# A fused four-layer kernel: in an attention turn, the second unit's values are weighed ahead of the last block's projection

## The chip, the cores and the metric

The kernel runs on one core of one Trainium2 chip. The metric is the device time in microseconds (us) of one execution, as the median of several runs. Three runs of the kernel before gave 1235.06, 1235.08 and 1236.01 us: a median of 1235.08 us. One further execution was recorded by the profiler; all rows below come from it.

The core has five engines that run their own instruction streams and meet only at semaphores: TensorE (PE in the rows; its weight loads are PEld), VectorE (DVE), ScalarE (ACT), GpSimd (POOL) and the queue of SyncE (SP).

## The reference, cut to what matters

The input x has 16 batches of 256 rows and 256 columns. It goes through four residual layers: a cross-attention to a context of 77 rows, a mixture of experts, a second cross-attention block with its own feed-forward part, and a last feed-forward layer. The change concerns the two attentions, which are computed by the same code. Of the first one:

```python
Q = _split_heads(q @ Wq.T + bq)      # q: layernorm(x), 16 heads of 16 columns
K = _split_heads(k @ Wk.T + bk)      # k, v: the context
V = _split_heads(v @ Wv.T + bv)
scores = jnp.einsum('bhnd,bhmd->bhnm', Q, K) / jnp.sqrt(jnp.float32(D))
scores = jnp.where(mask == 0, -jnp.inf, scores)
attn = jax.nn.softmax(scores, axis=-1)
out = jnp.einsum('bhnm,bhmd->bhnd', attn, V)
out = out.transpose(0, 2, 1, 3).reshape(q.shape[0], q.shape[1], H)
return out @ Wp.T + bp
...
x = x + jnp.tanh(g_xattn[0]) * _L0_xattn_ref(_layernorm(x, axis=-1), ctx_1024, ...)
```

## The kernel before, in words

An attention stage (stage 0 and stage 1) handles its 16 batches as 16 blocks of 256 rows, one after the other. The work of a block is cut into four units j = 0 to 3: one half of the heads (8 heads) by one half of the rows (128 rows). For each unit, TensorE multiplies queries with keys (`score`, L866), VectorE takes the maximum of each row and head (`score_max`, L471) and subtracts it (`less_max`, L476), ScalarE takes the exponential, TensorE transposes the probabilities (`transpose_prob`, L882), ScalarE copies the transposed ones out of PSUM (`transposed`, L724, the instruction of L728), TensorE weighs the values with them (`weigh_values`, L890), and VectorE divides by the sums (`normalise`, L485). When the four units of a block are done, TensorE transposes the result (`transpose_o`), ScalarE and VectorE split it in a high and a low part, TensorE multiplies it with the output weights (`project`, L912, twelve matmuls on L798 to L800), and VectorE adds the product to the residual stream (`residual`, L501: the instruction of L506 in stage 0, of L511 in stage 1).

The order of the work is written out by hand. There is one function `body` for each engine, run once for each block; I call one run a turn. The turns are software pipelined: turn b contains the four scores of block b, the end of block b-1 (its units 2 and 3, its projection and its residual) and the preparation of block b+1 (transposed input, keys, values, queries). The middle turns run in a loop of two turns per pass, an odd and an even one, so that some waits need an address computed first; the last three turns are written out. Turn 0 has no block behind it.

Two buffers tie the engines together around the change:

- `a.misc`, one PSUM bank, is used in turn for the transposed input, the keys and values, the queries and the projection's output. `transpose_x` (L841), which writes the next block's input there, waits on `y_done` (L848), the count of finished residuals. `keys_values` (L834) waits on `x_split`, which VectorE's `x_residue` (L427, the instruction of L429) raises after ScalarE's `x_rounded` (L695, the instruction of L698).
- `a.o_ps`, one PSUM bank, holds the weighed values of one unit. `weigh_values` waits on `pt_done`, which ScalarE's copy raises, and on `o_done` (L893), the count of finished normalisations.

The names in the rows: `s_a_kd` and `s_a_q_hi`, `s_a_q_lo` are keys and queries, `s_a_prob` and `s_a_prob_t` the probabilities and their transposes, `s_a_v_diagonal` the values, `s_a_o` the normalised output of a block, `s_a_xn` the normalised input, and `s_a_x_hi`, `s_a_x_lo` its two parts.

Of the kernel before, what the change touches and what calls it, by code (L numbers as in the profile page):

```python
# [85 lines left out]
def after(engine, semaphore, value):  # L86

    if not (isinstance(value, int) and value <= 0):
        engine.wait_ge(semaphore, value)
# [87 lines left out]
def flamingo_kernel(nc, d, out):  # L177
# [7 lines left out]
    with root:  # L185
# [206 lines left out]
        def attention_on_vector(dve, a, z_kept, additive_mask, tail=None, late=None):  # L392
            def weight_residue(n):
                part, i = WA_SPLIT[n]
                dve.wait_ge(a.w_round, 3 * a.stage + n + 1)
                dve.tensor_tensor(a.w_lo[:, part].rearrange("p k n -> p (k n)"), a.w_raw[:, i],
                                  a.w_hi[:, part].bitcast(F32).rearrange("p k n -> p (k n)"),
                                  ALU.subtract).then_inc(a.w_split, 1)
# [18 lines left out]
            def ln_apply(b):  # L417
                dve.wait_ge(a.ln_rstd, b.count + 1)
                after(dve, a.xt_ps, b.count)
                if a.stage == 1:  # L420
                    after(dve, a.ln_kept, b.count)
                for t in range(BT):
                    last = dve.tensor_scalar(a.xn[:, t, :], x[:, bass.ds(BT * b.n + t, 1), :].rearrange("p o c -> p (o c)"),
                                             a.mv[:, t, 0:1], a.rstd[:, t:t + 1], ALU.subtract, ALU.mult)
                last.then_inc(a.ln_done, 1)
# [26 lines left out]
            def keys(b):  # L452
                dve.wait_ge(a.k_round, key_step(a, b))
                key_residue(b.z, a.misc[:, 0:2 * CTXP]).then_inc(a.k_split, 1)
# [16 lines left out]
            def score_max(b, j):  # L471
                s, mx = scores_and_max(j)
                dve.wait_ge(a.scores_ps, UNITS * b.count + j + 1)
                dve.tensor_reduce(mx, s, AX.X, ALU.max).then_inc(a.max_done, 1)  # L474

            def less_max(b, j):  # L476
                u = UNITS * b.count + j
                s, mx = scores_and_max(j)
                dve.wait_ge(a.max_done, u + 1)
                after(dve, a.exp_done, u - 1)  # L480
                dve.tensor_tensor(a.prob[j % 2][:].rearrange("p (c h) n -> p c h n", c=2), s,  # L481
                                  mx.unsqueeze(3).broadcast_to([P, 2, HPC // 2, CTXP]),
                                  ALU.subtract).then_inc(a.scores_read, 1)

            def normalise(b, j):  # L485
                u = UNITS * b.count + j
                m, qt = j // BT, j % BT
                dve.wait_ge(a.pv_ps, u + 1)
                dve.reciprocal(a.row_sum[j % 2][:], a.o_ps[:, :, HD:HD + 1]).then_inc(a.sum_done, 1)
                dve.wait_ge(a.sum_done, u + 1)  # L490
                dve.tensor_tensor(a.o[b.z][:, qt, m * P:(m + 1) * P].rearrange("p (h n) -> p h n", n=HD),
                                  a.o_ps[:, :, 0:HD], a.row_sum[j % 2][:].broadcast_to([P, HPC, HD]),
                                  ALU.mult).then_inc(a.o_done, 1)
# [29 lines left out]
            def bias_of_output():  # L523

                dve.wait_ge(a.bias_step, 4 * a.stage + 2)
                dve.tensor_tensor(a.bias[:], a.bias_bank, a.bias[:], ALU.add).then_inc(a.bias_step, 1)
                if a.stage == 0:
                    dve.wait_ge(a.bias_step, 3)
                    dve.tensor_scalar(a.bias[:], a.bias[:], gates[:, 0:1], None, ALU.mult).then_inc(a.bias_step, 1)
# [62 lines left out]
            def body(b, behind, ahead):  # L592
                late_rows = a.stage == 1 and not behind
                if a.stage and ahead == 0:
                    ffn_norm(0)
                score_max(b, 0)
                less_max(b, 0)
                if not behind:
                    if a.stage == 0:
                        weight_residue(2)  # L600
                        dve.wait_ge(gates_done, 1)
                        dve.wait_ge(a.small_in, 32)
                        bias_of_output()
                    else:
                        ln_apply(second)
                if ahead:
                    x_residue(b.next())
                score_max(b, 1)
                if behind:
                    normalise(b.last(), 2)  # L610
                less_max(b, 1)
                if ahead > 1 and not late_rows:
                    ln_stats(b.next().next())
                if a.stage and ahead == 1:
                    ffn_stats()
                if a.stage and ahead == 0:
                    ffn_norm(1)
                if ahead > 1:
                    keys(b)
                if ahead:  # L620
                    value_tails(b.next())
                if behind:
                    normalise(b.last(), 3)
                score_max(b, 2)
                less_max(b, 2)
                if ahead > 1 and not late_rows:
                    ln_aggregate(b.next().next())
                if a.stage and ahead == 1:
                    ffn_aggregate()
                if behind:  # L630
                    o_residue(b.last())
                score_max(b, 3)
                if ahead:
                    q_residue(b.next())
                normalise(b, 0)
                less_max(b, 3)
                if late_rows:
                    ln_stats(second.next())
                    ln_aggregate(second.next())
                if a.stage and ahead == 0:  # L640
                    ffn_residue()
                if ahead > 1:
                    ln_apply(b.next().next())
                if behind:
                    residual(b.last())
                normalise(b, 1)

            paired_blocks(dve, BATCH, body, a.base, 3)
            final = Block(BATCH - 1, 1, (BATCH - 2) // 2, a.base)
# [154 lines left out]
        def attention_on_tensor(pe, a, last_of_mixture=None, ffn_transpose=None, ffn_up=None):  # L804
# [85 lines left out]
            def weigh_values(b, j):  # L890
                u = UNITS * b.count + j
                pe.wait_ge(a.pt_done, u + 1)
                after(pe, a.o_done, u)  # L893
                if j == 0:
                    after(pe, a.o_split, b.count)
                v = a.v_diagonal[b.z]
                pe.matmul(a.o_ps[:], a.prob_t[j % 2][:, PC - 1, :], v[:, j // BT, 1], start=True, stop=False, skip_group_check=True)  # L897
                for c in range(PC - 1):
                    last = pe.matmul(a.o_ps[:, 2 * c:2 * c + 2, :], a.prob_t[j % 2][:, c, :], v[:, j // BT, 0, 2 * c:2 * c + 2],  # L899
                                     start=False, stop=c == PC - 2, skip_group_check=True)  # L900
                last.then_inc(a.pv_ps, 1)
# [68 lines left out]
            def body(b, behind, ahead):  # L970
                score(b, 0)
                score(b, 1)
                if a.stage == 0 and not behind:
                    fold_bias()
                    pe.wait_ge(a.v_main, 1)
                    pe.wait_ge(a.v_tail, 1)
                if ahead:
                    transpose_x(b.next())
                if behind:
                    transpose_prob(b.last(), 3)  # L980
                    weigh_values(b.last(), 2)
                if ahead:
                    keys_values(b, ahead)
                if behind:
                    weigh_values(b.last(), 3)
                else:
                    pe.wait_ge(a.bias_step, 4 + 3 * a.stage)
                transpose_prob(b, 0)
                score(b, 2)
                score(b, 3)  # L990
                if behind:
                    transpose_o(b.last(), 0)
                if ahead:
                    queries(b.next())
                transpose_prob(b, 1)
                weigh_values(b, 0)
                transpose_prob(b, 2)
                if ffn_transpose and not ahead:
                    pe.wait_ge(a.scores_read, UNITS * 2 * BATCH - 1)
                    ffn_transpose()  # L1000
                if behind:
                    project(b.last(), ahead)
                else:
                    pe.wait_ge(a.w_split, 3 * (a.stage + 1))
                weigh_values(b, 1)

            paired_blocks(pe, BATCH, body, a.base, 3)
            final = Block(BATCH - 1, 1, (BATCH - 2) // 2, a.base)
# [2189 lines left out]
```

## Time and profile before

| | |
|---|---|
| median of three runs | 1235.08 us |
| the profiled execution, its own time | 1233.72 us |
| its span in the trace | 1232.0 us |
| TensorE matmuls, busy | 1160.3 us (94%) |
| TensorE weight loads, busy | 1085.2 us (88%) |
| VectorE, busy | 990.5 us (80%) |
| ScalarE, busy | 781.3 us (63%) |
| GpSimd, busy | 676.2 us (55%) |

The span runs from the first to the last instruction in the trace; the execution's own time is 1.72 us longer. The busy shares are sums over stages with different limits. Matmuls are pipelined: a matmul's record overlaps the next one's, so the distance from one start to the next, not the duration, tells how fast they go. A weight load stands ahead of each matmul, and its start is a good mark of when a group of matmuls begins. VectorE's records may overlap a little too.

### The profile page before, as it was taken

What the parts mean: (1) busy time and instruction counts of PE and PEld (TensorE: products, weight loads), DVE (VectorE), ACT (ScalarE), POOL (GpSimd) and SP (SyncE); (2) the same over time, 40 slices, a digit from 0 to 9 for tenths busy, and PEclk for the clock granted to TensorE, in tenths of its full rate; (3) what the DMA queues carried; (4) which work ended last, traced back from release to release, by engine and by line L of the source; (5) the groups of instructions that cost most, each with busy time, mean ns of one, the idle gap of its engine ahead of it and who ended that gap; (6) DMA issues with size and microseconds to landing.
All of it is one profiled execution on the core that took longest, in us unless ns stands there. A gap on an engine that the chain in (4) does not pass through costs nothing.

```text
span 1232.0 us, 26547 instructions
## 1 busy us (share of the span) xinstructions
PE 1160.3 (94%) x9040; PEld 1085.2 (88%) x9041; DVE 990.5 (80%) x2045; ACT 781.3 (63%) x1489; POOL 676.2 (55%) x772
## 2 busy tenths in 40 slices
PE   6999999989889999999699999998999999899998
PEld 5999999879778999999689999997899998788887
DVE  6899999756897766666689999996987887888887
ACT  4777777668464555555377777775444546777874
POOL 5444333243105556553788777721454656788885
PEclk9999999979999999999899999999999999999999
DMA  4211121113102333333543333313000000000001
GB/s 129 56 53 53 53 57 57 46 61 112 52 1 61 109 106 109 104 105 97 130 74 66 68 67 62 62 30 103 5 2 0 0 0 1 9 18 26 26 26 35
DMA packets 70276, 68.74 MB, mean 56 GB/s; under 512 B 24576, under 2 KB 62208, under 8 KB 69952
## 3 DMA queue, kind: packets, MB, share of 16 engines
q1 hardware_dynamic: 55920, 47.77, 12.8%
q0 software_dynamic: 12576, 18.62, 8.1%
q10 hardware_dynamic: 1712, 1.50, 0.4%
q8 instruction: 36, 0.59, 0.2%
q14 instruction: 32, 0.26, 0.1%
HBM read 44.00 MB, written 18.61 MB: 51 GB/s over the span
## 4 chain that ended last, share of the span: by engine, by line
PE 74%; DVE 11%; ACT 5%; issue 5%; POOL 4%; DMA 1%; ACTq 0%; DVEq 0%; POOLq 0%; SPq 0%
PE PSUM L798 13%; PE PSUM L800 13%; PE PSUM L799 13%; PE PSUM L899 8%; PE PSUM L887 6%; PE PSUM L878 5%; PE PSUM L897 2%; POOL s_t_gh L2659 2%; PE PSUM L810 2%; PE PSUM L851 1%; PE PSUM L908 1%; PE PSUM L1959 1%; ACT s_m_xn L1456 1%; PE PSUM L2848 1%; PE PSUM L2849 1%
## 5 line engine op out<-in xcount | busy, mean ns | idle before, releaser
L2209 POOL TENSOR_TENSOR s_f_h_lo<-s_f_h,s_f_h_hi 128x512 fp32r<-128x512 f32 x64 | 93.4, 1466 | 102.9 <-ACT s_f_h_hi L2153 102.3
L1382 POOL DMA_INDIRECT s_m_tile_x<-normed_x,s_tokens x78 | 96.8, 1241 | 75.1 <-DVE s_tokens L1673 53.7
L899 PEld LDWEIGHTS PSUM<-s_a_v_diagonal,s_a_prob_t 128*128 128x128 f32 x1024 | 125.9, 192 | 0.0
L899 PE MATMUL PSUM<-s_a_v_diagonal,s_a_prob_t 128*128 128x36 f32 x1024 | 125.2, 268 | 0.0
L728 ACT ACTIVATE s_a_prob_t<-PSUM 128x640 f32<-128x640 f32 x128 | 90.0, 703 | 36.6 <-PE PSUM L887 34.9
L474 DVE TENSOR_REDUCE s_a_row_max<-PSUM 128x8 f32<-128x640 f32 x128 | 104.7, 818 | 7.3 <-PE PSUM L878 4.0
L481 DVE TENSOR_TENSOR s_a_less<-PSUM,s_a_row_max 128x640 f32<-128x640 f32 x128 | 104.9, 820 | 4.4
L1049 POOL DMA_INDIRECT s_x<-sorted_y,s_slots x60 | 95.3, 1588 | 19.7 <-issue 13.6
L2147 ACT ACTIVATE s_f_h<-PSUM,s_cols 128x512 f32<-128x512 f32 x64 | 44.0, 688 | 89.6 <-PE PSUM L800 89.0
L887 PE MATMUL PSUM<-s_ident,s_a_prob 128*128 128x128 f32 x640 | 93.7, 277 | 1.0
L798 PE MATMUL PSUM<-s_m_x_hi,s_m_up_w 128*128 128x256 f32 x312 | 91.8, 294 | 1.1 <-issue 1.0
L2659 POOL TENSOR_TENSOR s_t_gh<-s_t_h,s_t_g 128x1024 f32<-128x1024 f32 x31 | 79.2, 2556 | 17.8 <-ACT s_t_h L2595 17.3
L799 PE MATMUL PSUM<-s_m_x_hi,s_m_up_w 128*128 128x256 f32 x312 | 88.3, 283 | 0.0
L800 PE MATMUL PSUM<-s_m_x_lo,s_m_up_w 128*128 128x256 f32 x312 | 88.2, 283 | 0.0
L721 ACT ACTIVATE PSUM<-s_a_mask 128x640 f32<-128x640 f32 (+1 forms) x128 | 86.5, 691 | 0.0
L711 ACT ACTIVATE s_a_prob<-s_a_less 128x512 f32<-128x512 f32 x128 | 80.5, 629 | 8.8 <-DVE s_a_less L481 7.2
L878 PE MATMUL PSUM<-s_a_kd,s_a_q_hi 64*128 64x320 f32 x512 | 76.5, 341 | 7.0 <-DVE s_a_q_lo L436 4.7
L887 PEld LDWEIGHTS PSUM<-s_ident,s_a_prob 128*128 128x128 f32 x640 | 74.1, 146 | 3.9 <-issue 1.5
L798 PE MATMUL PSUM<-s_ffn_hi,s_f_h_hi 128*128 128x256 f32 x256 | 73.5, 287 | 1.1 <-POOL s_f_h_lo L2209 1.1
L800 PE MATMUL PSUM<-s_ffn_lo,s_f_h_hi 128*128 128x256 f32 x256 | 72.8, 284 | 0.0
L799 PE MATMUL PSUM<-s_ffn_hi,s_f_h_lo 128*128 128x256 f32 x256 | 72.6, 284 | 0.0
L1504 ACT ACTIVATE s_m_h<-PSUM,s_m_bias 128x256 f32<-128x256 f32 x78 | 32.7, 470 | 60.6 <-PE PSUM L800 60.6
(327 smaller groups left out, 4222.5 us busy)
## 6 DMA issues: line engine op xcount, KB each, us to landing
sorted_y<-s_m_tile_y SPq DMA_DIRECT2D x39, 256.0 KB
s_a_kd<-s_a_k_parts SPq DMA_DIRECT2D x126, 40.0 KB
s_x<-x SPq DMA_DIRECT2D x16, 256.0 KB, 3.1
s_a_ctx<-ctx SPq DMA_DIRECT2D x32, 128.0 KB, 2.8
s_moe_raw<-moe_w SPq DMA_DIRECT2D x16, 256.0 KB
normed_x<-s_m_xn SPq DMA_DIRECT2D x16, 256.0 KB, 3.1
y<-s_x SPq DMA_DIRECT2D x16, 256.0 KB, 2.1
s_late_raw<-moe_w SPq DMA_DIRECT2D x11, 256.0 KB, 2.9
```

The source lines that it names most:

```text
L474: dve.tensor_reduce(mx, s, AX.X, ALU.max).then_inc(a.max_done, 1)
L481: dve.tensor_tensor(a.prob[j % 2][:].rearrange("p (c h) n -> p c h n", c=2), s, mx.unsqueeze(3).broadcast_to([P, 2, HPC // 2, CTXP]), ALU. ...
L798: pe.matmul(ps, lh, rh, start=start and i == 0, stop=False, skip_group_check=not start)
L799: pe.matmul(ps, ll, rh, start=False, stop=False, skip_group_check=not start)
L800: last = pe.matmul(ps, lh, rl, start=False, stop=stop and i == n - 1, skip_group_check=not start)
L878: last = pe.matmul(ps, queries[i][rows, m, qt * P:(qt + 1) * P], keys[i][rows, m], start=False, stop=i == 2, skip_group_check=True)
L887: last = pe.transpose(a.prob_t_ps[:, c, :], a.pairs[j % 2][:, c, :], ident[:])
L899: last = pe.matmul(a.o_ps[:, 2 * c:2 * c + 2, :], a.prob_t[j % 2][:, c, :], v[:, j // BT, 0, 2 * c:2 * c + 2], start=False, stop=c == PC - ...
L1049: last = pool.indirect_dma_start(x[:, tile, :], None, d["sorted_y"], row, compute_op=ALU.add)
L1382: pool.indirect_dma_start(m.tile_x[n % 2][:, t, :], None, d["normed_x"], bass.IndirectOffsetOnAxis(ap=tokens[:, BT * n + t:BT * n + t + 1] ...
L2209: pool.tensor_tensor(f.h_lo[m % 4][:], f.h[m % 4][:], f.h_hi[m % 4][:].bitcast(F32), ALU.subtract).then_inc(f.h_split, 1)
L2659: pool.tensor_tensor(w.gh[t % 2][:], w.h[t % 2][:], w.g2[:], ALU.mult).then_inc(w.gh_done, 1)
```

## The change

In `body` on TensorE, `weigh_values(b, 1)` is moved from behind the projection of the last block to ahead of it. In `body` on VectorE, `normalise(b, 1)` is moved from behind the residual of the last block to ahead of it, so that VectorE takes the two results in the order in which TensorE makes them. ScalarE, GpSimd and SyncE have the same instructions in the same order as before. No instruction is added or removed, and no wait is changed.

```diff
@@ attention_on_vector, body
                 if ahead > 1:
                     ln_apply(b.next().next())
+                normalise(b, 1)
                 if behind:
                     residual(b.last())
-                normalise(b, 1)
@@ attention_on_tensor, body
+                weigh_values(b, 1)
                 if behind:
                     project(b.last(), ahead)
                 else:
                     pe.wait_ge(a.w_split, 3 * (a.stage + 1))
-                weigh_values(b, 1)
```

On TensorE, at the end of an odd turn of the loop, this stood in a row before (L887 is the transposing of unit 2, L798 to L800 the projection, L897 and L899 the weighing of unit 1, L878 the first score of the next turn):

```order
L887 MATMUL PSUM<-s_ident,s_a_prob 128x128 x4
L798 MATMUL PSUM<-s_a_w_hi,s_a_o_hi 128x256 [waits a_q_split,a_o_split]
L799 MATMUL PSUM<-s_a_w_hi,s_a_o_lo 128x256
L800 MATMUL PSUM<-s_a_w_lo,s_a_o_hi 128x256
...
L897 MATMUL PSUM<-s_a_v_diagonal,s_a_prob_t 128x144 [waits a_o_done,a_pt_done]
L899 MATMUL PSUM<-s_a_v_diagonal,s_a_prob_t 128x36 x4
L869 ISA
L871 ISA [waits a_q_split,a_kd_in0]
L878 MATMUL PSUM<-s_a_kd,s_a_q_hi 128x320 [waits a_masked]
```

And this stands there now:

```order
L887 MATMUL PSUM<-s_ident,s_a_prob 128x128 x4
L897 MATMUL PSUM<-s_a_v_diagonal,s_a_prob_t 128x144 [waits a_o_done,a_pt_done]
L899 MATMUL PSUM<-s_a_v_diagonal,s_a_prob_t 128x36 x4
L798 MATMUL PSUM<-s_a_w_hi,s_a_o_hi 128x256 [waits a_q_split,a_o_split]
L799 MATMUL PSUM<-s_a_w_hi,s_a_o_lo 128x256
L800 MATMUL PSUM<-s_a_w_lo,s_a_o_hi 128x256
...
L869 ISA
L871 ISA [waits a_q_split,a_kd_in0]
L878 MATMUL PSUM<-s_a_kd,s_a_q_hi 128x320 [waits a_masked]
```

The weighing, with its waits on `o_done` and `pt_done`, moved ahead of the twelve matmuls of the projection. Behind the scores, TensorE's next group is `transpose_x` (L851), which waits on `y_done`, in both kernels.

On VectorE, at the same place in stage 0 (L423 is the next but one block's normalised input, L489 and L491 the normalisation of unit 1, L506 the residual, L474 the first maximum of the next turn):

```order
 L418 REGISTER_ALU
 L423 TENSOR_SCALAR s_a_xn<-s_x,s_a_mv,s_a_rstd 128x256 x2
+L489 RECIPROCAL s_a_row_sum<-PSUM 128x8
+L491 TENSOR_TENSOR s_a_o<-PSUM,s_a_row_sum 128x128
 L506 ISA
 L506 SCALAR_TENSOR_TENSOR s_x<-PSUM,s_gates,s_x 128x512
-L489 RECIPROCAL s_a_row_sum<-PSUM 128x8
-L491 TENSOR_TENSOR s_a_o<-PSUM,s_a_row_sum 128x128
 L473 ISA
 L474 TENSOR_REDUCE s_a_row_max<-PSUM 128x8
```

The residual moved from ahead of the normalisation to the last place of the turn, directly ahead of the next turn's first maximum.

## Rows read from the trace of the kernel before

**Rows 1.** The page: span, and busy time of each engine.
```profile
span 1232.0 us, 26547 instructions
PE 1160.3 (94%) x9040; PEld 1085.2 (88%) x9041; DVE 990.5 (80%) x2045; ACT 781.3 (63%) x1489; POOL 676.2 (55%) x772
```
**Rows 2.** The chain that ended last, window 100 to 117 us, shares by line.
```profile
by line: PE PSUM L899 23.9%; PE PSUM L887 19.1%; PE PSUM L878 12.7%; PE PSUM L798 8.9%; PE PSUM L800 8.2%; PE PSUM L799 8.2%; PE PSUM L897 7.2%; PE PSUM L810 4.6%; PE PSUM L908 3.4%; PE PSUM L851 3.4%; issue 0.5%
```
**Rows 3.** Busy time in one turn of stage 0, residual to residual; then stage 0's end.
```profile
core 0: us, PE busy (x) PEld busy (x) DVE busy (x) ACT busy (x) POOL busy (x), PEclk, DMA share, GB/s
89.24:103.48 14.24, 14.19 (x129) 13.51 (x127) 13.11 (x31) 10.89 (x24) 5.76 (x8) 1.00 0.15 36
...
249.00:262.00 13.00, 8.66 (x45) 7.65 (x44) 7.16 (x28) 6.92 (x13) 8.26 (x30) 0.65 0.23 81
```
**Rows 4.** Timeline of TensorE's weight loads: start, duration, line, what, count.
```profile
101.18 0.53 PEld L887 LDWEIGHTS PSUM<-s_ident,s_a_prob 128*128 128x128 f32 x5
101.67 0.19 PEld L798 LDWEIGHTS PSUM<-s_a_w_hi,s_a_o_hi 128*128 128x128 f32 x1
...
103.05 0.30 PEld L897 LDWEIGHTS PSUM<-s_a_v_diagonal,s_a_prob_t 128*128 128x128 f32 x2
103.28 0.98 PEld L899 LDWEIGHTS PSUM<-s_a_v_diagonal,s_a_prob_t 128*128 128x128 f32 x8
104.31 0.19 PEld L878 LDWEIGHTS PSUM<-s_a_kd,s_a_q_hi 64*128 64x128 f32 x2
...
105.39 0.42 PEld L851 LDWEIGHTS PSUM<-s_ident,s_a_xn 128*128 128x128 f32 x4 [0.19 <-issue]
...
107.65 0.43 PEld L810 LDWEIGHTS PSUM<-s_a_ctx,s_a_w_raw 128*128 128x128 f32 x3
```
**Rows 5.** Timeline of VectorE over the same stretch.
```profile
100.50 0.88 DVE L436 SCALAR_TENSOR_TENSOR s_a_q_lo<-PSUM,s_cols,s_a_q_hi 128x256 fp32r<-128x256 f32 x2 [0.16 <-ACT s_a_q_hi L703]
101.30 0.20 DVE L489 RECIPROCAL s_a_row_sum<-PSUM 128x8 f32<-128x8 f32 x1
101.53 0.29 DVE L491 TENSOR_TENSOR s_a_o<-PSUM,s_a_row_sum 128x128 f32<-128x128 f32 x1
...
103.48 0.75 DVE L506 SCALAR_TENSOR_TENSOR s_x<-PSUM,s_gates,s_x 128x512 f32 x1 [0.28 <-PE PSUM L800]
104.42 0.21 DVE L489 RECIPROCAL s_a_row_sum<-PSUM 128x8 f32<-128x8 f32 x1 [0.19 <-PE PSUM L899]
...
105.07 0.82 DVE L474 TENSOR_REDUCE s_a_row_max<-PSUM 128x8 f32<-128x640 f32 x1
106.01 0.82 DVE L481 TENSOR_TENSOR s_a_less<-PSUM,s_a_row_max 128x640 f32<-128x640 f32 x1
106.75 0.68 DVE L429 TENSOR_TENSOR s_a_x_lo<-PSUM,s_a_x_hi 128x512 fp32r<-128x512 f32 x1
107.35 0.81 DVE L474 TENSOR_REDUCE s_a_row_max<-PSUM 128x8 f32<-128x640 f32 x1
```
**Rows 6.** Timeline of ScalarE over the same stretch.
```profile
100.36 0.70 ACT L728 ACTIVATE s_a_prob_t<-PSUM 128x640 f32<-128x640 f32 x1
...
106.08 0.60 ACT L698 ACTIVATE s_a_x_hi<-PSUM 128x512 fp32r<-128x512 f32 x1 [1.45 <-PE PSUM L851]
```
**Rows 7.** Timeline of VectorE, the turn before (the other turn of the loop).
```profile
89.24 0.75 DVE L506 SCALAR_TENSOR_TENSOR s_x<-PSUM,s_gates,s_x 128x512 f32 x1 [0.28 <-PE PSUM L800]
...
92.56 0.69 DVE L429 TENSOR_TENSOR s_a_x_lo<-PSUM,s_a_x_hi 128x512 fp32r<-128x512 f32 x1
```
**Rows 8.** Timeline of TensorE's weight loads, same turn as the group before.
```profile
93.30 0.43 PEld L810 LDWEIGHTS PSUM<-s_a_ctx,s_a_w_raw 128*128 128x128 f32 x3
```
**Rows 9.** Timeline of VectorE in stage 1.
```profile
728.45 0.69 DVE L511 TENSOR_TENSOR s_z_sum<-PSUM,s_z_sum 128x512 f32 x1 [0.17 <-PE PSUM L800]
...
731.72 0.68 DVE L429 TENSOR_TENSOR s_a_x_lo<-PSUM,s_a_x_hi 128x512 fp32r<-128x512 f32 x1
```
**Rows 10.** Timelines at stage 0's last turn: VectorE, then TensorE's weight loads.
```profile
245.95 0.29 DVE L491 TENSOR_TENSOR s_a_o<-PSUM,s_a_row_sum 128x128 f32<-128x128 f32 x1
246.36 0.30 PEld L897 LDWEIGHTS PSUM<-s_a_v_diagonal,s_a_prob_t 128*128 128x128 f32 x2 [0.35 <-issue]
```

## The prediction

> **What bounds the kernel now.** I read the page's busy times first. TensorE is busy 94% of the span, VectorE 80% [rows 1]; these are means over all stages, so they say nothing of one stage. The turns come next. In stage 0 one turn, residual to residual, takes 14.24 us, in which TensorE's matmuls cover 14.19 us and VectorE works 13.11 us, at a granted clock of 1.00 [rows 3]. The chain of waits over such a stretch is all TensorE lines and 0.5% issue [rows 2]. The reader should see that TensorE sets the pace, but that VectorE has only about 1.1 us of slack in a turn, part of it in cracks too small to use. So the question is not only what TensorE gains, but whether VectorE's work stays in time.
>
> The timelines of the two engines show where they touch. TensorE's keys (L810) start at 107.65 us [rows 4]; VectorE's x_residue, which they wait for, runs from 106.75 to 106.75 + 0.68 = 107.43 us [rows 5]. So the keys start 0.22 us behind it. In the other turn of the loop x_residue ends at 92.56 + 0.69 = 93.25 us [rows 7] and the keys start at 93.30 us [rows 8], 0.05 us behind. In both turns x_residue ends hardly before TensorE needs it. This chain (residual, maximum, subtraction, x_residue, keys) is already as late as it may be.
>
> **The change, step 1: the weighing moved forward.** Before, it starts behind the projection and waits for nothing. Now it would start where the projection starts now, at 101.67 us [rows 4]. It waits for two releases. The ScalarE copy is done at 100.36 + 0.70 = 101.06 us [rows 6]: in time. The normalisation of unit 0 ends at 101.53 + 0.29 = 101.82 us [rows 5]: late. How long from such an end to TensorE's next load? The same copy's end at 101.06 us releases the loads of L887 at 101.18 us [rows 4, 6], 0.12 us; the bounds are the 0.05 and 0.22 us of the keys. I take 0.12 us, as that group also waits for two semaphores: the weighing starts at 101.94 us, a new stall of 0.27 us. The stall can't be worked off by a faster TensorE, because the normalisation is on a chain of ScalarE and VectorE work: VectorE's L436 just ahead of it already waits 0.16 us for ScalarE [rows 5], and that chain begins with TensorE's own queries. Queued behind this wait are the projection and the next scores.
>
> **Step 2: the residual comes later.** The weighing takes 2 + 8 loads; from 103.05 us, eight loads that cover 0.98 us begin at 103.28 us with 0.11 us between them, so it occupies 0.23 + 8 x 0.11 = 1.1 us [rows 4]. From the projection's first load to the residual's start is 103.48 - 101.67 = 1.81 us [rows 4, 5]. The residual starts at 101.94 + 1.1 + 1.81 = 104.85 us instead of 103.48 us: 1.37 us later, relative to everything that came before in the turn.
>
> **Step 3: what is given back.** Before, VectorE waits for the scores after the residual: the normalisation comes between, and the maximum starts at 105.07 us, 1.59 us behind the residual's start [rows 5]. Now the normalisation runs under the projection (free from about 103.3 to 104.8 us), and the maximum follows the residual directly. VectorE's records overlap when nothing is waited for: L429 ends at 107.43 us and the next starts at 107.35 us, 0.08 us earlier [rows 5]. So the maximum starts 0.75 - 0.08 = 0.67 us behind the residual's start. From there to x_residue it is 106.75 - 105.07 = 1.68 us as before. Hence residual to x_residue shrinks from 3.27 to 0.67 + 1.68 = 2.35 us: 0.92 us given back. The scores don't hold it: before, the first score begins at 104.31 us and its maximum at 105.07 us, 0.76 us later [rows 4, 5]; now the scores begin at about 104.5 us and their maximum would be possible at 105.3 us, while VectorE comes at 104.85 + 0.67 = 105.52 us.
>
> The other way to x_residue is through `transpose_x`, which waits for the residual's end: 0.75 us, 0.12 us release, 106.08 - 105.39 = 0.69 us to ScalarE's rounding and its 0.60 us [rows 4, 6] give 2.16 us, under 2.35 us. So VectorE's way ends last, with little in it. Through the scores TensorE itself would reach the keys about 3.0 us behind the residual's start; x_residue allows them at 2.35 + 0.68 + 0.22 = 3.25 us in the one turn and some 3.1 us in the other. Therefore the seam between projection and scores, wherever it got shorter, lies under this wait and brings nothing.
>
> **Step 4: the sum.** A stage 0 turn grows by 1.37 - 0.92 = 0.45 us. In stage 1 the residual takes 0.69 us and x_residue starts 731.72 - 728.45 = 3.27 us behind it [rows 9]; now 0.61 + 1.68 = 2.29 us, so 0.98 us is given back and a turn grows by 0.39 us. From turn 1 to turn 14 there are 13 such passages in each stage: 13 x 0.45 + 13 x 0.39 = 10.9 us. The passage into the last turn has no transpose_x, so only the stall counts, about 0.3 us per stage. In the last turn TensorE pays the stall once more, but the wait of the final weighing goes: there L897 starts at 246.36 us, 0.12 us behind the normalisation's end at 245.95 + 0.29 = 246.24 us, after 0.35 us of idle [rows 10]. I count these two as cancelling. All: 10.9 + 0.6 = 11.5 us. The profiled execution has a span of 1232.0 us and its own time of 1233.72 us, so 1.72 us around it; with the change 1245.2 us. The median of the runs shown is 1.36 us above that execution, which gives 1246.6, in round numbers **1247 us**.
>
> **Bounds.** Release to weighing, 0.05 to 0.22 us instead of 0.12: -2 to +3 us over 28 turns. Residual to maximum: the row nearest to it is L429 to L474, 0.08 us overlap, which I take; the other end is a gap of 0.12 us, as between the end of the maximum at 105.89 and L481 at 106.01 us [rows 5]: +0.2 us x 26 = +5 us. Below, if VectorE's way had another 0.2 us in it that I don't see (the keys then start with TensorE's own 3.0 us), -5 us.
>
> The Trainium skill, page "VectorE: DVE Perf Modes", section "The DRAIN you can't avoid", says that the next VectorE operation does not start until the pipe is empty. By that rule the maximum would start 0.75 us behind the residual, 0.08 us later, and the sum would be 2 us larger. The rows show the overlap of 0.08 us [rows 5]; I go by them.
>
> **Rivals.**
> A. *Faster.* TensorE is the bound, so what counts are its seams. From the last load of the weighing, about 103.28 + 7 x 0.11 = 104.05 us, a load would follow at 104.16; the score's comes at 104.31 us [rows 4], 0.15 us lost. If this goes and the normalisation is in time, 28 x 0.15 = 4 us are won: 1231 us. For it: TensorE's share [rows 3]. Against it: the normalisation's end at 101.82 us and the wait on y_done. It decides only if the weighing starts at 101.7 us. The Trainium skill, page "Perfetto Trace Analysis", section "Matmul Optimizations", speaks for this side: it asks that matmuls execute back-to-back in batches.
> B. *Only the stall.* VectorE's way stays hidden, each turn costs step 1 alone: 28 x 0.27 = 7.5 us, 1242.5 us. For it: VectorE's idle time before residual and normalisation, 0.28 and 0.19 us [rows 5]. Against it: the keys' margin of 0.05 us in one turn.
> C. *No change.* The stall takes the place of waits TensorE has anyway (0.19 us before transpose_x [rows 4], 0.2 us before the keys): 1235 to 1236 us. Against it: these lie behind the residual, which is itself later.
> D. *More.* VectorE has no overlap and its lateness runs on through the turn to the next normalisation, which then holds the weighing longer: 0.65 us per turn, 28 x 0.65 = 18 us, 1253 us. For it: VectorE's 13.11 us of 14.24.
> E. *The clock.* At stage 0's end, where TensorE is busy only 8.66 of 13.00 us, the granted clock is 0.65 of full, a mix of 2.4 and 1.2 GHz; in the turns it is 1.00 [rows 3]. If the new gaps brought 1.5 us of lost time in every other turn, 1247 + 20 = 1267 us. Gaps of 0.3 to 0.4 us in 14.7 are far from that row. The Trainium skill, page "TensorE: Matmul & The Clock Gate", section "A second HAM failure mode: psum-queue depth-cycling", tells of a kernel whose short idles between groups made the clock swing.
>
> **How the numbers follow.** Forecast 0.64, A 0.05, B 0.12, C 0.06, D 0.11, E 0.02. The range 1240.5 to 1254 us holds the forecast with its bounds, B and most of D. Faster by over 0.2% is A, 0.05; within 0.2% (2.5 us, about what a measurement of this kernel can tell from no change) is C and a small part of B, 0.07; slower 0.88.
>
> **What would show it.** In the changed kernel's timeline of a middle turn of stage 0: L897 starts about 0.12 us behind the end of L491, with some 0.25 us between the transposes and it; L506 starts 1.8 us behind the projection's first load and the maximum of L474 0.67 us behind L506; transpose_x's first load comes some 0.87 us behind L506's start; the keys stay bound to x_residue's end; the turn is 14.7 us long and the clock 1.00. I am wrong if the weighing follows the transposes without a gap (then A), or if the turn is 14.5 us with keys that start well behind x_residue's end (B), or if the idle time before L436 vanishes and the stall at L897 exceeds 0.4 us (D).

## The result, and the profile after

The changed kernel takes 1252.24 us (median of six runs, 1249.47 to 1258.29), the kernel before on the same chip 1235.45 us (1234.63 to 1236.01). The ratio is 1.0135, with a 95% interval of 1.0103 to 1.0166. In a second comparison on another occasion the same kernel took 1248.08 us (ten runs, 1245.55 to 1261.97) against 1236.07 us: a ratio of 1.0117 (1.0075 to 1.0159). It is slower by 1.2 to 1.4%, inside the forecast range of 1240.5 to 1254 us, and 1 us (second comparison) to 5 us (first) above the forecast of 1247 us.

First the turn that answers to [rows 4 to 6]: an odd turn's end in the loop of stage 0, in the changed kernel. TensorE's weight loads:

```profile
104.24 0.30 PEld L897 LDWEIGHTS PSUM<-s_a_v_diagonal,s_a_prob_t 128*128 128x128 f32 x2 [0.23 <-issue]
104.47 0.98 PEld L899 LDWEIGHTS PSUM<-s_a_v_diagonal,s_a_prob_t 128*128 128x128 f32 x8
105.37 0.19 PEld L798 LDWEIGHTS PSUM<-s_a_w_hi,s_a_o_hi 128*128 128x128 f32 x1
...
106.63 0.19 PEld L800 LDWEIGHTS PSUM<-s_a_w_lo,s_a_o_hi 128*128 128x128 f32 x1
106.94 0.19 PEld L878 LDWEIGHTS PSUM<-s_a_kd,s_a_q_hi 64*128 64x128 f32 x2
...
108.04 0.42 PEld L851 LDWEIGHTS PSUM<-s_ident,s_a_xn 128*128 128x128 f32 x4 [0.21 <-issue]
...
110.41 0.57 PEld L810 LDWEIGHTS PSUM<-s_a_ctx,s_a_w_raw 128*128 128x128 f32 x4 [0.23 <-issue]
```

VectorE over the same stretch:

```profile
102.81 0.88 DVE L436 SCALAR_TENSOR_TENSOR s_a_q_lo<-PSUM,s_cols,s_a_q_hi 128x256 fp32r<-128x256 f32 x2 [0.17 <-ACT s_a_q_hi L703]
...
103.83 0.29 DVE L491 TENSOR_TENSOR s_a_o<-PSUM,s_a_row_sum 128x128 f32<-128x128 f32 x1
...
105.60 0.21 DVE L489 RECIPROCAL s_a_row_sum<-PSUM 128x8 f32<-128x8 f32 x1
105.84 0.29 DVE L491 TENSOR_TENSOR s_a_o<-PSUM,s_a_row_sum 128x128 f32<-128x128 f32 x1
107.17 0.75 DVE L506 SCALAR_TENSOR_TENSOR s_x<-PSUM,s_gates,s_x 128x512 f32 x1 [1.03 <-PE PSUM L800]
107.84 0.81 DVE L474 TENSOR_REDUCE s_a_row_max<-PSUM 128x8 f32<-128x640 f32 x1
108.77 0.82 DVE L481 TENSOR_TENSOR s_a_less<-PSUM,s_a_row_max 128x640 f32<-128x640 f32 x1
109.52 0.68 DVE L429 TENSOR_TENSOR s_a_x_lo<-PSUM,s_a_x_hi 128x512 fp32r<-128x512 f32 x1
110.11 0.81 DVE L474 TENSOR_REDUCE s_a_row_max<-PSUM 128x8 f32<-128x640 f32 x1
```

Three things are to be seen. The weighing (L897) starts at 104.24 us, 0.12 us behind the end of unit 0's normalisation (103.83 + 0.29 = 104.12), after idle time that the view lists as 0.23 us: the new stall. VectorE, which before waited 0.28 us ahead of the residual [rows 5], now waits 1.03 us there, because the projection ends the turn; the work that it used to do behind the residual's start, the maximum and what follows, still stands behind it. And the keys (L810) start 0.21 us behind x_residue's end (109.52 + 0.68 = 110.20), as before (in the other turn 0.06 us, 95.60 us against 94.86 + 0.68 = 95.54 us): the same chain ends last, only later. Its idle time of 0.23 us at L810 is new; before, TensorE had work until shortly before.

The turn itself, residual to residual, and then the last layer, in the changed kernel:

```profile
92.51:107.16 14.65, 14.56 (x128) 13.51 (x128) 12.98 (x30) 10.89 (x23) 5.78 (x8) 1.00 0.21 52
1069.00:1245.00 176.00, 161.93 (x1046) 142.15 (x1045) 147.08 (x255) 123.26 (x138) 139.81 (x157) 0.95 0.06 21
```

The turn that answers to [rows 3] has grown from 14.24 to 14.65 us at a clock of 1.00. The second row is a stretch in which not one instruction was changed; its granted clock is 0.95. The same stretch in the trace of the kernel before, and in the second trace of the changed kernel:

```profile
1054.00:1230.00 176.00, 161.56 (x1098) 141.76 (x1096) 147.52 (x267) 125.36 (x140) 141.59 (x162) 1.00 0.07 23
```
```profile
1070.00:1245.00 175.00, 159.30 (x1066) 139.01 (x1064) 145.64 (x262) 122.16 (x137) 137.22 (x161) 0.99 0.07 25
```

So the first trace of the changed kernel (1258.29 us, the longest of its six runs) holds a loss in its last layer that the second (1246.48 us) doesn't.

### The profile page after: what moved, and what is told of

It is laid out like the page before. It is cut to its first block, busy times and chain, and to the rows that moved or that the text cites. A ratio compares the mean times of both kernels' runs of the same rounds, so it can differ in the third digit from the quotient of the medians.

```text
span 1256.5 us, 26547 instructions
## 1 busy us (share of the span) xinstructions
PE 1180.9 (94%) x9040; PEld 1096.2 (87%) x9041; DVE 993.8 (79%) x2045; ACT 781.0 (62%) x1489; POOL 678.9 (54%) x772
## 4 chain that ended last, share of the span: by engine, by line
PE 75%; DVE 12%; ACT 5%; issue 4%; POOL 2%; DMA 1%; ACTq 0%; DVEq 0%; SPq 0%; POOLq 0%
PE PSUM L798 13%; PE PSUM L800 12%; PE PSUM L799 12%; PE PSUM L899 8%; PE PSUM L887 6%; PE PSUM L878 5%; PE PSUM L897 3%; PE PSUM L810 2%; PE PSUM L2848 2%; PE PSUM L851 1%; PE PSUM L908 1%; PE PSUM L2849 1%; PE PSUM L1959 1%; DVE s_t_x_lo L2728 1%; PE PSUM L2882 1%
## 5 line engine op out<-in xcount | busy, mean ns | idle before, releaser
L899 PEld LDWEIGHTS PSUM<-s_a_v_diagonal,s_a_prob_t 128*128 128x128 f32 x1024 | 126.6, 193 | 0.0
L899 PE MATMUL PSUM<-s_a_v_diagonal,s_a_prob_t 128*128 128x36 f32 x1024 | 125.9, 269 | 0.0
L474 DVE TENSOR_REDUCE s_a_row_max<-PSUM 128x8 f32<-128x640 f32 x128 | 104.5, 816 | 6.4 <-PE PSUM L878 6.3
L887 PE MATMUL PSUM<-s_ident,s_a_prob 128*128 128x128 f32 x640 | 95.2, 281 | 1.3 <-ACT s_a_prob_t L728 0.2
L798 PE MATMUL PSUM<-s_m_x_hi,s_m_up_w 128*128 128x256 f32 x312 | 91.8, 294 | 1.1 <-issue 1.0
L800 PE MATMUL PSUM<-s_m_x_lo,s_m_up_w 128*128 128x256 f32 x312 | 88.2, 283 | 0.0
L878 PE MATMUL PSUM<-s_a_kd,s_a_q_hi 64*128 64x320 f32 x512 | 77.2, 345 | 6.5 <-DVE s_a_q_lo L436 4.7
L887 PEld LDWEIGHTS PSUM<-s_ident,s_a_prob 128*128 128x128 f32 x640 | 75.3, 148 | 4.2 <-issue 2.2
L798 PE MATMUL PSUM<-s_ffn_hi,s_f_h_hi 128*128 128x256 f32 x256 | 73.4, 287 | 1.1 <-POOL s_f_h_lo L2209 1.1
L800 PE MATMUL PSUM<-s_ffn_lo,s_f_h_hi 128*128 128x256 f32 x256 | 72.7, 284 | 0.0
L798 PE MATMUL PSUM<-s_moe_w,s_m_h_hi 128*128 (+1 forms) x220 | 64.3, 292 | 8.8 <-DVE s_x L1704 4.8
```

The lines of the kernel that those rows point to most:

```text
L798: pe.matmul(ps, lh, rh, start=start and i == 0, stop=False, skip_group_check=not start)
L800: last = pe.matmul(ps, lh, rl, start=False, stop=stop and i == n - 1, skip_group_check=not start)
L878: last = pe.matmul(ps, queries[i][rows, m, qt * P:(qt + 1) * P], keys[i][rows, m], start=False, stop=i == 2, skip_group_check=True)
L887: last = pe.transpose(a.prob_t_ps[:, c, :], a.pairs[j % 2][:, c, :], ident[:])
```

## The experiments

Turn lengths below are means over twelve turns of stage 0, from the first to the thirteenth start of the residual (L506). In before: 46.27 to 217.48 us, 14.27 us; in the changed kernel 48.34 to 224.73 us, 14.70 us. A granted clock of 0.98 over a span means that for about 4% of it TensorE had the lower of its two clocks; this is the time at half clock below. Beside the first run of the changed kernel, before took 1235.45 us; beside its second run, the two halves and the divided projection 1236.07 us (25 runs); beside the last four kernels of the table 1235.67 us (25 runs). The rows from which two of the turn lengths come, of before and of the kernel with TensorE's half alone:

```profile
L506 DVE SCALAR_TENSOR_TENSOR s_x<-PSUM,s_gates,s_x x13: 750/751/751, 46.3 to 217.5; 128x512 f32 x12, 128x512 f32<-128x512 f32 x1
```
```profile
L506 DVE SCALAR_TENSOR_TENSOR s_x<-PSUM,s_gates,s_x x13: 750/750/751, 49.8 to 232.4; 128x512 f32 x12, 128x512 f32<-128x512 f32 x1
```

| kernel | stage 0 turn | stage 1 turn | median, us | ratio to before (95%) | span of its trace, clock |
|---|---|---|---|---|---|
| before | 14.27 | 14.29 | 1236.07 and 1235.67 | | 1232.0, 0.981 |
| changed | 14.70 | 14.65 | 1252.24 | 1.0135 (1.0103 to 1.0166) | 1256.5, 0.970 |
| changed, again | 14.70 | 14.66 | 1248.08 | 1.0117 (1.0075 to 1.0159) | 1244.7, 0.981 |
| TensorE's half | 15.22 | 15.19 | 1266.06 | 1.0209 (1.0142 to 1.0277) | 1265.3, 0.973 |
| VectorE's half | 14.70 | 14.69 | 1250.12 | 1.0108 (1.0076 to 1.0139) | 1250.1, 0.971 |
| weighing inside the projection | 14.47 | 14.42 | 1241.95 | 1.0038 (1.0009 to 1.0066) | 1235.8, 0.981 |
| swap in stage 0 alone | 14.69 | 14.29 | 1242.94 | 1.0055 (1.0037 to 1.0072) | 1241.1, 0.978 |
| thin residual | 14.57 | 14.60 | 1246.92 | 1.0104 (1.0057 to 1.0152) | 1240.2, 0.982 |
| before, started later | 14.26 | 14.30 | 1240.74 | 1.0041 (1.0016 to 1.0067) | 1241.0, 0.977 |
| before, context waits first | 14.21 | 14.24 | 1236.76 | 0.9996 (0.9979 to 1.0013) | 1235.9, 0.977 |

**The changed kernel once more.** No edit.

> The changed kernel itself, once more, with a trace of its own. What I want to know: in the first trace the turns grew as predicted (15 us in all up to the last layer) and 9.6 us more were lost in the last layer, at a granted clock of 0.95 there instead of 1.00. Theory 'turns': the turns again take 14.7 us in stage 0 and 14.65 us in stage 1, and the loss up to the last layer is again 13 to 15 us. Theory 'clock is by chance': the last layer's loss differs from run to run, 0 to 10 us, and the time lies anywhere from 1248 to 1258 us. Rival, 'the swap itself reaches the last layer': its loss is 9 to 10 us again.

The turns agree to 0.02 us with the first trace. The last layer's loss is 0.7 us instead of 9.6. The theory of the turns holds, and the rival that the swap costs 9 to 10 us in the last layer in every execution falls. That the changed kernel meets such a loss more often than before isn't excluded: three of its ten runs here took 1258.62 to 1261.97 us, over 10 us above their median, where one of the 25 runs of before beside them did (1248.94 us), and none of these was traced.

**TensorE's half alone.**

```diff
@@ attention_on_tensor, body (VectorE as before)
+                weigh_values(b, 1)
                 if behind:
                     project(b.last(), ahead)
                 else:
                     pe.wait_ge(a.w_split, 3 * (a.stage + 1))
-                weigh_values(b, 1)
```

> Only TensorE's half: the weighing ahead of the projection, while VectorE still does the residual ahead of the normalisation of unit 1. My theory (residual, maximum, subtraction, x_residue, keys is the chain that ends last): the residual starts 1.39 us later as in the changed kernel, and the normalisation now stands behind it, so the next maximum starts 1.2 us behind the residual instead of 0.67: a turn of 14.7 + 0.5 = 15.2 us, 13 us above the changed kernel, some 1262 us. Rival (TensorE and its new stall alone set the turn, VectorE is hidden): the same turn as the changed kernel, 14.7 us, 1252 us.

The turn: forecast 15.2 us, measured 15.22 us. The time is 1266.06 us (four runs, 1261.66 to 1270.07), 4 us above the forecast of 1262 us. VectorE in this kernel, then TensorE's keys:

```profile
110.85 0.75 DVE L506 SCALAR_TENSOR_TENSOR s_x<-PSUM,s_gates,s_x 128x512 f32 x1 [1.69 <-PE PSUM L800]
111.52 0.20 DVE L489 RECIPROCAL s_a_row_sum<-PSUM 128x8 f32<-128x8 f32 x1
111.75 0.29 DVE L491 TENSOR_TENSOR s_a_o<-PSUM,s_a_row_sum 128x128 f32<-128x128 f32 x1
111.96 0.81 DVE L474 TENSOR_REDUCE s_a_row_max<-PSUM 128x8 f32<-128x640 f32 x1
...
113.64 0.68 DVE L429 TENSOR_TENSOR s_a_x_lo<-PSUM,s_a_x_hi 128x512 fp32r<-128x512 f32 x1
```
```profile
114.53 0.19 PEld L810 LDWEIGHTS PSUM<-s_a_ctx,s_a_w_raw 128*128 128x128 f32 x1 [0.66 <-issue]
```

The maximum starts 1.11 us behind the residual, where it was 0.67 us in the changed kernel; the keys come 3.68 us behind the residual instead of 3.24 us. TensorE has the same order of work in both, so a VectorE that is hidden can't explain 0.52 us per turn: the chain through VectorE ends last. VectorE's half of the change is what keeps the price at 0.43 us.

**VectorE's half alone.**

```diff
@@ attention_on_vector, body (TensorE as before)
+                normalise(b, 1)
                 if behind:
                     residual(b.last())
-                normalise(b, 1)
```

> Only VectorE's half: the normalisation of unit 1 ahead of the residual, TensorE in the order of before. There is no new stall at the weighing and no later projection. My theory: VectorE waits for the weighing at the turn's end (104.42 us in the trace of before), normalises to 104.95 us, and only then does the residual, so the next maximum starts at 105.54 instead of 105.07 us: 0.47 us per turn, 26 turns, 12 us: 1247 us. Rival (the stall of the weighing is the cost): no change, 1235 us.

Measured 14.70 us a turn, 0.43 us more than before (forecast 0.47), and a time of 1250.12 us (forecast 1247). Its rows, VectorE and then TensorE's loads:

```profile
106.62 0.21 DVE L489 RECIPROCAL s_a_row_sum<-PSUM 128x8 f32<-128x8 f32 x1 [1.22 <-PE PSUM L899]
106.86 0.29 DVE L491 TENSOR_TENSOR s_a_o<-PSUM,s_a_row_sum 128x128 f32<-128x128 f32 x1
107.07 0.74 DVE L506 SCALAR_TENSOR_TENSOR s_x<-PSUM,s_gates,s_x 128x512 f32 x1
107.72 0.81 DVE L474 TENSOR_REDUCE s_a_row_max<-PSUM 128x8 f32<-128x640 f32 x1
...
109.40 0.68 DVE L429 TENSOR_TENSOR s_a_x_lo<-PSUM,s_a_x_hi 128x512 fp32r<-128x512 f32 x1
```
```profile
107.93 0.42 PEld L851 LDWEIGHTS PSUM<-s_ident,s_a_xn 128*128 128x128 f32 x4 [0.53 <-issue]
...
110.33 0.19 PEld L810 LDWEIGHTS PSUM<-s_a_ctx,s_a_w_raw 128*128 128x128 f32 x1 [0.25 <-issue]
```

There is no stall at the weighing here, and TensorE does its work in the order of before; moving one residual behind one normalisation on VectorE costs as much as the whole swap. The transposing of the next input (L851) waits for the residual's end (107.07 + 0.74 = 107.81, 0.12 us later), with 0.53 us of idle where before had 0.19 [rows 4]. The keys again start behind x_residue's end, by 0.25 us (110.33 against 109.40 + 0.68 = 110.08 us). The rival that only the weighing's stall costs time is out.

**The weighing between the two halves of the projection.**

```diff
@@ attention_on_tensor, on top of the changed kernel
-            def project(b, ahead):
+            def project(b, ahead, between=None):
...
                 for t in range(BT):
+                    if t and between:
+                        between()
...
-                weigh_values(b, 1)
                 if behind:
-                    project(b.last(), ahead)
+                    project(b.last(), ahead, lambda: weigh_values(b, 1))
...
```

> The changed kernel, but the weighing stands between the two halves of the projection (six matmuls ahead of it, six behind). The normalisation of unit 0 is then done before TensorE gets to the weighing, so the stall of 0.27 us goes; the residual is still late by the weighing and one more change from the one to the other kind of matmul, 1.2 us, of which VectorE gives back 0.93. My theory: a turn of 14.27 + 0.3 = 14.55 us, 1235.4 + 26 x 0.25 = 1242 us. Rival (the stall is all the cost): 1235 us. Rival (the stall costs nothing, the lateness of the residual all): 14.65 us, 1250 us.

The time came out as forecast, 1241.95 us, and the turn a little better, 14.47 us instead of 14.55. In its timeline the loads run through without a gap:

```profile
103.04 0.19 PEld L800 LDWEIGHTS PSUM<-s_a_w_lo,s_a_o_hi 128*128 128x128 f32 x1
103.15 0.30 PEld L897 LDWEIGHTS PSUM<-s_a_v_diagonal,s_a_prob_t 128*128 128x128 f32 x2
```

So 0.23 us of the swap's 0.43 us per turn goes with the stall, and 0.20 us is the residual's lateness that isn't given back: the weighing takes 104.29 - 103.15 = 1.14 us between the two halves, and VectorE gives 0.92 us back, which leaves 0.22 us. The "one more change of the matmul's kind" that the expectation counted costs nothing here: the loads on either side of the weighing follow it as they do elsewhere.

**The swap in the first attention alone.**

```diff
@@ attention_on_tensor, body: the new order where a.stage == 0, else that of before; VectorE's body alike
+                if a.stage == 0:
+                    weigh_values(b, 1)
                 if behind:
                     project(b.last(), ahead)
...
+                if a.stage != 0:
+                    weigh_values(b, 1)
```

> The swap in the first attention stage alone, the second as before. My theory (a fixed price per turn): stage 0's turns take 14.70 us, stage 1's 14.29 us as before; the time is 1236 + 13 x 0.44 + 1 = 1243 us, about half of the changed kernel's loss. Rival (the loss is made after the attentions, through the granted clock in the later layers): the later layers' loss does not split by stage, and the time is 1236 or 1248 us by chance.

14.69 and 14.29 us, 1242.94 us: a price per turn in the stage that has the swap, 7.3 us of the 12 us of both, and none in the other. Behind stage 1's last residual (L511) this trace takes 375.4 us, that of before 375.5 us: the rival that the loss is made in the later layers falls for this execution.

**A thin residual.**

```diff
@@ attention_on_vector, residual, on top of the changed kernel
-                    dve.scalar_tensor_tensor(tiles(b), y, gates[:, 0:1], tiles(b), ALU.mult,
+                    dve.scalar_tensor_tensor(tiles(b)[:, :, 0:16], y[:, :, 0:16], gates[:, 0:1], tiles(b)[:, :, 0:16], ALU.mult,
```

> The changed kernel with the residual cut to 32 of its 512 columns (the rest of the residual and so most of the attention's output is left out); the semaphores stay. Theory 'residual is the bound': its 0.75 us leaves the chain whole, the keys move 0.6 us forward, and a turn takes 14.7 - 0.6 = 14.1 us: 1232 us. Theory of the prediction, with its own numbers: once the residual is gone, the first score's end comes last, 0.53 us behind the residual's start against 0.67 us now, so only 0.1 to 0.15 us per turn come back: a turn of 14.57 us, 1246 us. Theory 'VectorE is the bound through the whole turn': 14.1 us too, and the wait of L436 for ScalarE grows.

This kernel leaves out most of the residual, in stage 1 (L511) as in stage 0, and so most of the attention's output. Stage 0's turn is the forecast 14.57 us. Stage 1's turn is 14.60 us, only 0.05 us less than in the changed kernel. The time of 1246.92 us says little, since the four runs lie between 1241.95 and 1254.82 us.

```profile
106.37 0.25 DVE L506 SCALAR_TENSOR_TENSOR s_x<-PSUM,s_gates,s_x 128x32 f32 x1 [1.04 <-PE PSUM L800]
106.89 0.82 DVE L474 TENSOR_REDUCE s_a_row_max<-PSUM 128x8 f32<-128x640 f32 x1 [0.27 <-PE PSUM L878]
```

VectorE now waits for the score (L878), and the maximum starts 0.52 us behind the residual. Of the 0.50 us taken off the residual only 0.13 us came back in stage 0. The residual's own length is thus only a small part of what the swap costs: with the projection last, the next score's end is nearly as late as the residual's.

**The kernel before, started later.**

```diff
@@ gpsimd, and the counts that wait on pool_const raised by LATE = 4
+            for n in range(LATE):
+                pool.memset(a0.kd[0][:].bitcast(F32), 0.0).then_inc(pool_const, 1)
+                pool.wait_ge(pool_const, n + 1)
             pool.memset(ident[:], 0.0).then_inc(pool_const, 1)
```

> The kernel before, with four memsets of 1.3 us put ahead of everything on GpSimd, so that all engines start about 5.5 us later; nothing else is changed. Theory 'the granted clock in the later layers depends on where they fall after the start': spells of 0.5 move or appear in the last layer, and the time differs from 1236 + 5.5 by several us. Rival 'spells come by chance at the stage borders, whatever the start': 1241 us, as many us at half clock as before (49), give or take one spell.

1240.74 us, 5.07 us above its before, where the trace shows that 4.9 us were added, not the 5.5 us of the expectation: GpSimd's first memset of before starts at 0.80 us there and at 5.69 us here. Its trace has 60 us at half clock, a spell of which lies in the last layer (granted clock 0.99 there), against 49 us in the trace of before. This speaks for spells that come in some executions and not in others rather than for a time after the start on which they depend, but one trace doesn't settle it.

Their places in the work are not random: three traces have a spell in the last layer, and its start lies 29 us behind that layer's first matmul (L2833) in each: 1080.9 - 1051.4 us here, 1087.2 - 1058.1 and 1084.5 - 1055.2 us in the two of the changed kernel. In the 7.2 to 7.4 us ahead of that place TensorE is busy for 5.19 us in the first trace of the changed kernel and for 5.20 us in that of before, and the granted clock falls to 0.50 in the one and stays at 1.00 in the other.

That long runs occur without the swap is shown by the 25 runs of before in the second comparison, of which one took 1248.94 us and another 1241.68 us, around a median of 1236.07, and by one of the ten runs of the kernel started later (1251.67 us); of the 25 runs of before beside it the longest took 1242.28 us.

**The kernel before, with the context's waits first.**

```diff
@@ attention_on_tensor, keys_values
+                if ahead > 1 and b.z == 0:
+                    for z in range(2):
+                        pe.wait_ge(a.ctx_in[z], 16 * (b.half + a.base // 2 + 2))
                 pe.wait_ge(a.x_split, b.count + 2)
@@ keys(b): the same waits removed
```

> The kernel before, with the waits for the context (a semaphore raised by a DMA long before, with an address computed in between) ahead of the wait for x_residue in every even turn. In the traces the keys start 0.22 us behind x_residue's end in the even turns and 0.05 us in the odd ones. My theory: the even turns' keys then start 0.05 us behind it too, each even turn gets up to 0.15 us shorter, 12 of them: 0 to 2 us less than before, 1234 to 1236 us. Rival: the wait is not the cause, the keys keep 0.22 us.

```profile
106.50 0.68 DVE L429 TENSOR_TENSOR s_a_x_lo<-PSUM,s_a_x_hi 128x512 fp32r<-128x512 f32 x1
```
```profile
107.30 0.19 PEld L810 LDWEIGHTS PSUM<-s_a_ctx,s_a_w_raw 128*128 128x128 f32 x1
```

The keys start 0.12 us behind x_residue's end in the even turns, not 0.22 us and not the forecast 0.05 us: of the two steps that TensorE's queue had between the end and the load, the address and a second wait, the address went. The turn is 0.06 us shorter in the trace, 14.21 against 14.27 us. In the time nothing can be told: 1236.76 us, a ratio of 0.9996 (0.9979 to 1.0013).

## Why the prediction was right, point by point

**What bounds a turn.** The claim was that TensorE sets the pace but that the chain residual, maximum, subtraction, x_residue, keys is as late as it may be. The two halves show it: VectorE's half alone, with TensorE's order untouched, costs 0.43 us per turn, and TensorE's half alone 0.95 us.

**Step 1, the stall.** Predicted 0.27 us, by a release of 0.12 us; the trace shows the 0.12 us, and taking the stall away gave back 0.23 us per turn. From the last load of the transposes, at 103.87 us, to the weighing's first at 104.24 us it is 0.37 us; less the usual 0.11 us that is a stall of 0.26 us.

**Step 2, the late residual.** From the weighing's first load to the residual: predicted 1.1 + 1.81 = 2.91 us, measured 107.17 - 104.24 = 2.93 us.

**Step 3, what is given back.** Residual to maximum 0.67 us (107.84 - 107.17), residual to x_residue 2.35 us (109.52 - 107.17), the keys at 3.24 us, and the first load of transpose_x 0.87 us behind the residual (108.04 - 107.17): all as worked out. With the thin residual the maximum could follow the score's end 0.52 us behind the residual's start. The expectation of that run had 0.53 us; the prediction's own numbers, 105.3 - 104.85 = 0.45 us, had the scores a little too early, because the seam between projection and scores costs 0.31 us. The overlap of 0.08 us stands here too: the maximum starts at 107.84 us, the residual ends at 107.92. The Trainium skill, page "VectorE: DVE Perf Modes", section "The DRAIN you can't avoid", says that the next VectorE operation waits for an empty pipe, and also that one that is not held back starts earlier. The prediction took only the first of the two; these two operations, with no wait left open between them, overlap by 0.08 us, so the second is the one that this case's rows bear out.

**Step 4, the sum.** Per passage 0.45 us predicted and 0.43 us measured in stage 0, 0.39 and 0.35 to 0.37 us in stage 1. Against the trace of before, the second trace of the changed kernel grew by 12.7 us in span (1244.7 - 1232.0), where 11.5 us were summed up. It splits so: 2.8 us up to the first residual (by the prediction's 1.37 us, half of it step 2; the granted clock from 10 to 46 us is 0.91 against 0.95 before), 5.9 us from there to stage 0's last residual, -0.1 us in the mixture, 3.4 us in stage 1, and 0.8 us in the two layers behind it.

The sum had 13 x 0.45 + 0.3 = 6.2 us for stage 0 and 13 x 0.39 + 0.3 = 5.4 us for stage 1, and nothing ahead of the first residual. So stage 0 is right, stage 1 came out 2.0 us too dear, because its last two turns got 1.5 us shorter where 0.3 us more had been counted, and the 2.8 us at the start were missed; that 12.7 us lie so near 11.5 us is partly luck. In time that execution took 1246.48 us, the forecast for it was 1245.2 us.

**What was missed.** The median of the first six runs lies 5 us above the forecast. The turns don't hold these 5 us; they are the same in both traces. The first trace has 76 us at half clock, the second 50 us, the trace of before 49 us, and 1256.5 - 1244.7 = 11.8 us lie between the two spans: 8.9 us in the last layer, 2.7 us in the mixture and 1.2 us in stage 1, less 0.8 us at the start. The six runs go with their mean granted clock: 1258.29 and 1255.95 us at 0.970, 1251.43 at 0.972, 1253.06 at 0.973, 1251.03 at 0.974 and 1249.47 us at 0.977. The term of the sum that was off is its last one: I took the clock outside the turns as that of the one profiled execution of before, as if it were fixed. Rival E had the clock fall in the turns; there it stayed at 1.00. Whether the slower kernel meets more such spells than before, or only met them by chance in that comparison, stays open. For more of them speak the three long runs of ten in the second comparison; the median there is 12 us above before, of which the two stages (5.9 and 3.4 us) and step 2 at the start explain most.

**The rivals.** A is shown wrong, and in its sign: the seam between projection and score is not shorter than the one it replaces. From the projection's last load at 106.63 us to the score's first at 106.94 us it is 0.31 us; a load follows every 0.11 us otherwise, so 0.2 us is lost. Before, the weighing's last load is at 104.07 us in the trace (the prediction took 104.05) and the score's first at 104.31 us, so 0.13 us was lost. And the weighing didn't follow the transposes without a gap, which A needed. B (only the stall) is refuted by VectorE's half. C would need the stall to take the place of TensorE's other waits; these stayed, 0.21 us at L851, and 0.23 us at L810 came on top. D (lateness that runs on through the turn) didn't happen: L436 still waits for ScalarE, 0.17 us in the turn shown, so VectorE catches up in each turn.

## What to carry to other kernels

When a consumer's order must follow a producer's, look at what the consumer does next: a result moved to the end of a turn puts its consumer directly ahead of the next turn's first work, and idle time in front of it (here 1.03 us of VectorE) is no cover for what now stands behind it. Two engines that are each a few per cent from the bound can't be judged by which one is busier; follow the chain between them from row to row and add it up, once per turn. And a kernel whose clock moves by itself outside the changed part needs several traces before the last few microseconds are given a cause.

## What the runs showed of the hardware that I had not expected

- Two groups of matmuls put side by side don't always run on without a gap: from the projection on 128 rows to the score on 64 rows, the distance between loads is 0.31 us (0.32 us in the kernel with the divided projection, 104.88 to 105.20 us), where loads within a group stand 0.11 us apart. The last thing that the score waits for in these turns, ScalarE's mask, had ended 0.6 us before (0.4 us in the other kernel). From the projection to the weighing, both on 128 rows, it is 0.11 us (103.04 to 103.15 us), no gap at all. What makes the difference isn't shown: the two groups differ in rows and in how their waits are built.
- The distance from an end on VectorE to TensorE's load depends on how the wait is built: 0.05 us where the weight load waits by itself (the keys in odd turns), 0.12 us with a second wait ahead of it (the weighing), 0.22 us where an address is computed and a second semaphore waited for in between (the keys in even turns). The last fell to 0.12 us when the waits were put in another order.
- The time at half clock differs between executions of one and the same kernel, 76 and 50 us. The spells lie at the borders of stages, in the mixture and in the two last layers, at the same places of the work in several traces. In the middle turns of the two attentions, from the first to the thirteenth residual, the clock was 1.00 in all ten traces.
